# A four-layer graph network on one core: the scatters of the second edge sort dealt out over three stages, and the pair counting split differently between VectorE and ScalarE

## The chip, the cores and the metric

The kernel runs on one core of a Trainium2 chip. The metric is device time in microseconds (us), lower is better. Before the change three runs gave 10820.09, 10835.07 and 10841.47 us, median 10835.07 us.

The core has engines that run side by side and meet at semaphores: PE (TensorE, matrix products; its weight loads stand in a row of their own, PEld), DVE (VectorE), ACT (ScalarE), POOL (GpSimd) and SP (SyncE, which here only issues DMAs). POOL issues the indirect DMAs, in which a column of 128 indices in on-chip memory names the DRAM row of each of 128 elements. An indirect DMA that writes so is a scatter, one that reads so is a gather.

## The reference

The graph has 3125 nodes and 103,125 edges (50,000 random ones, their reverses, and a loop for each node). Four layers follow each other, each on relu(layer norm(x)), each added to x:

```python
edge_index = jnp.stack([src, dst])
x = x + L0(relu(layernorm(x)), ..., edge_index, edge_type_64)    # attention with a relation per edge, softmax over edges of one src
x = x + L1(relu(layernorm(x)), edge_index, ...)                  # 3 graph attention layers, softmax over edges of one dst
x = x + L2(relu(layernorm(x)), src, dst, ...)                    # 2 graph convolutions, then two small dense layers
x = x + L3(relu(layernorm(x)), ..., src, dst, edge_type_474)     # attention with a relation per edge, softmax over edges of one dst
```

In L1 each layer computes, for 4 heads,

```python
e = leaky_relu(alpha_s[src] + alpha_d[dst], 0.2)
alpha = softmax of e over the edges of one dst
out = segment_sum(xs[src] * alpha, dst) + b
```

and in L2 a convolution is `segment_sum(h[src], dst)`, with degrees as scales and a weight matrix. L1 and L2 need of the edges only how often each pair (node, node) occurs. L0 and L3 need the edges themselves, L0 sorted by src and L3 by dst.

## The kernel before, in words

Nodes are held as 25 blocks of 128 (`NB = 25`), edges as 816 tiles of 128 (`z.tiles = 816`). The program is a row of stages; between two stages all engines meet.

**Sorting (`group_edges`).** For each edge and for each of the two sorts q = 0 and 1 the place in a padded list of edges is worked out. For q = 0 POOL scatters the edges in the same stage (L244: 816 scatters of 128 elements of 8 bytes into `ells[0]`). For q = 1 the places only go to DRAM (`position_dram`), and `ells[1]` is filled later. `ells[1]` is first read in the last stage, L3.

**Counting (`count_pairs`).** It makes the 3200 x 3200 matrix of how often each pair of nodes has an edge, from `ells[0]`, and the logarithm of it, and writes both to DRAM (`counts`, `logs`). It goes over 13 pairs of node blocks (`PAIRS`), with buffer `p % 2` for pair p. For one pair and one group of 64 edge slots (in this run each pair has one group):

- DVE splits the ids into low and high parts (L1206 to L1215), PE transposes them, ACT copies them to `splitT` (L1131).
- DVE compares the high parts with 0..24 (`hi_hot`, L1220) and, for eight chunks of 16 rows, the low parts with 0..127 (`lo_hot`, L1224). In both the value from `splitT` is repeated along the innermost dimension.
- PE multiplies the one-hots of a chunk, 32 matmuls of 64 rows (L1107); DVE adds the product from PSUM to `counts[k]` (L1233), whose destination has a step of 256 elements innermost. POOL has cleared `counts[k]` before (L1075).
- PE then turns the counts of the pair in 50 transposes (L1088), ACT copies those out (L1138, 14 copies), sends them to DRAM (L1142), takes the logarithm (L1146) and, once DVE has clamped it (`tell`, L1243), sends `logs` (L1151).

The order is written out by hand. On ACT it is: `splitT` of pair p, copies and logarithm of pair p, `logs` of pair p - 1. On DVE: pair p + 1, then `tell(p)`. On PE: pair p, then turning pair p.

**L0.** It reads `ells[0]`; POOL gathers rows for it without pause. The change does not touch it.

**Attention layers (`graph_attention`, L1).** Three layers of 25 node blocks. POOL gathers the `logs` rows of a block (L1675, 1.6 MB into one of two buffers), which may start when DVE is through with the block two before. Then, for the first 68 of the 75 blocks, it issues 12 scatters of the second sort (L1682, `PART = 12`, 68 x 12 = 816); SP loads their indices and payload two parts ahead (L1660, L1661). DVE needs the `logs` of a block before it starts on it: for each of 4 heads one pass over 3200 elements that adds and takes the maximum (L1848) and one that adds the logs and finds the peak (L1852), which the trace names CUSTOM_DVE_ANT_0. ACT takes the exponentials (L1771) and copies what PE has transposed (L1779).

**Convolutions (`graph_convolution`, L2).** Twice PE multiplies the features by the count matrix (L2008), of which SP loads 25 blocks of 1.6 MB through a ring of four (L1983). POOL scatters x at the start (L704), waits until the first convolution has gone to DRAM (`second_out`), and gathers it in another order (L711).

## Time and profile before

The profiled execution took 10830.81 us, of which the span of the profile is 10829.0 us and 1.8 us lie around it. TensorE's mean granted clock is 0.77. Stages, from the same trace (busy us of each engine):

| stretch, us | stage | length | PE | DVE | ACT | POOL |
|---|---|---|---|---|---|---|
| 0 to 1493 | sorting | 1493 | 1076 | 1200 | 498 | 907 |
| 1493 to 2210 | counting | 717 | 182 | 570 | 164 | 76 |
| 2300 to 6020 | L0 | 3720 | 2330 | 2755 | 2291 | 2743 |
| 6150 to 8840 | attention layers, blocks | 2690 | 1876 | 2180 | 2056 | 2079 |
| 8895 to 9040 | first sum over the count matrix | 145 | 132 | 0 | 0 | 17 |
| 9115 to 9260 | second sum | 145 | 138 | 6 | 0 | 0 |
| 9330 to 10829 | L3 and output | 1499 | 906 | 1115 | 703 | 950 |

How to read it: a stage's busy engine is not by itself its bound. What ends the waits of that engine is asked of the waits and of the timeline. The page's own chain of waits names only the last hundredths of the span here, as all engines meet between stages.

### The profile page before, as it was taken

The numbers are of one execution on the slowest core, as the hardware profiler recorded it, in microseconds if no ns is written. First come the engines' busy times: TensorE is split into PE (matmuls) and PEld (weight loads), VectorE is DVE, ScalarE is ACT, GpSimd is POOL, SyncE is SP. The second block draws the span as 40 slices with busy tenths as digits, with TensorE's granted clock in tenths as the row PEclk, the third lists the DMA queues.
The fourth block names the chain that finished last, engine by engine and source line by source line (L and its number), as shares of the span: only waits on it lengthen the run. The fifth ranks groups of instructions, "written<-read, shape, count | busy, mean of one in ns | idle before, by whom it ended". The sixth has DMA issues, their size and how long they took to land. (4 is left out here: it accounts for less than half of the span.)

```text
span 10829.0 us, 223526 instructions
## 1 busy us (share of the span) xinstructions
PE 6746.9 (62%) x64938; PEld 5475.7 (51%) x64939; DVE 7986.2 (74%) x22059; ACT 5754.5 (53%) x12392; POOL 6921.5 (64%) x5770
## 2 busy tenths in 40 slices
PE   3984952236666566656666467676676668466665
PEld 2973952235554454545555355455554544366665
DVE  9779778847777677767777678778787870477776
ACT  4224222236666566646666477767777760155554
POOL 0777731057776777767777488868868710466665
PEclk8555555568887788778888798889898889777777
DMA  0111114322223223223222211111111126322222
GB/s 22 57 37 28 60 36 144 124 62 53 52 53 48 49 53 53 52 45 52 53 53 53 39 49 43 49 43 45 49 37 49 49 86 249 73 48 46 46 45 44
DMA packets 420007, 630.47 MB, mean 58 GB/s; under 512 B 273511, under 2 KB 330305, under 8 KB 396201
## 3 DMA queue, kind: packets, MB, share of 16 engines
q0 software_dynamic: 192432, 385.10, 17.0%
q1 hardware_dynamic: 160080, 158.87, 4.7%
q10 hardware_dynamic: 67401, 85.32, 2.2%
q8 instruction: 50, 0.82, 0.0%
q14 instruction: 44, 0.36, 0.0%
HBM read 527.43 MB, written 103.02 MB: 58 GB/s over the span
## 5 line engine op out<-in xcount | busy, mean ns | idle before, releaser
L895 POOL DMA_INDIRECT l_land<-table,l_words x3744 | 3596.3, 961 | 1342.5 <-issue 1158.6
L1682 POOL DMA_INDIRECT ell<-gat_stage_pay,gat_stage_at x816 | 1929.5, 2365 | 248.6 <-issue 248.6
L1365 PE MATMUL left_product_ps<-k_w,messageT 128*128 128x128 f32 x5616 | 1045.5, 343 | 530.2 <-ACT messageT L1400 530.2
L1365 PEld LDWEIGHTS left_product_ps<-k_w,messageT 128*128 128x128 f32 x5616 | 881.4, 239 | 736.6 <-ACT messageT L1400 736.6
L2231 PE MATMUL rel_ps<-relation_parts,hot 128*128 128x128 bf16 x11328 | 831.1, 248 | 414.8 <-DVE hot L2330 414.8
L1779 ACT COPY gat_probT<-gat_ps 128x512 f32<-128x512 f32 (+1 forms) x2100 | 1026.5, 550 | 112.8 <-PE gat_ps L1722 100.1
L2231 PEld LDWEIGHTS rel_ps<-relation_parts,hot 128*128 128x128 bf16 x11328 | 810.7, 114 | 436.2 <-DVE hot L2330 436.2
L244 POOL DMA_INDIRECT ell<-pay,position x816 | 842.4, 1032 | 289.3 <-issue 280.0
L1359 PE MATMUL left_turned_ps<-ident,message 128*128 128x128 f32 x2808 | 560.2, 334 | 725.4 <-DVE message L1491 725.4
L1722 PE MATMUL gat_ps<-ident,gat_logit 128*128 128x128 f32 x3750 | 629.7, 307 | 605.1 <-ACT gat_logit L1771 589.7
L1416 ACT ACTIVATE weighed<-kept,l_prob 128x128 f32 x2784 | 888.9, 391 | 59.1 <-ACT l_prob L961 59.0
L1722 PEld LDWEIGHTS gat_ps<-ident,gat_logit 128*128 128x128 f32 x3750 | 462.8, 155 | 765.1 <-ACT gat_logit L1771 618.3
L1359 PEld LDWEIGHTS left_turned_ps<-ident,message 128*128 128x128 f32 x2808 | 387.2, 173 | 826.7 <-DVE message L1491 823.7
L295 PE MATMUL looked_ps<-count,loT_wide 128*128 (+1 forms) x3264 | 755.6, 384 | 47.8 <-issue 44.8
L1351 PE MATMUL rel_ps<-relation_parts,hotT 128*128 128x256 bf16 x4248 | 777.3, 335 | 2.0 <-ACT hotT L1395 2.0
L295 PEld LDWEIGHTS looked_ps<-count,loT_wide 128*128 128x128 f32 x3264 | 744.7, 333 | 56.7 <-issue 54.2
L1412 ACT ACTIVATE right<-left_product_ps 128x512 f32<-128x512 f32 x702 | 418.1, 596 | 622.0 <-DVE l_score L1552 363.4
L1771 ACT ACTIVATE gat_logit<-gat_logit,gat_peak 128x1536 f32<-128x1536 f32 (+1 forms) x300 | 487.0, 1624 | 417.1 <-DVE gat_peak L1852 416.7
L1728 PE MATMUL gat_ps<-gat_probT,h 128*32 128x128 f32 x15000 | 706.4, 282 | 0.1
L981 DVE TENSOR_REDUCE part<-weighed 128x128 f32<-128x1024 f32 x348 | 667.2, 1917 | 27.1
L1722 PE MATMUL gat_ps<-ident,work 128*128 128x128 f32 x3750 | 574.9, 284 | 178.8 <-ACT work L1771 156.3
L1552 DVE CUSTOM_DVE_ANT_0 product<-right,left_now 128x128 f32<-128x128 f32 x2784 | 625.3, 288 | 8.6
(332 smaller groups left out, 15741.2 us busy)
## 6 DMA issues: line engine op xcount, KB each, us to landing
gcn_edges<-counts SPq DMA_DIRECT2D x50, 1600.0 KB, 8.1
l_land<-table,l_words POOLq DMA_INDIRECT x3744
rows<-low_dram SPq DMA_DIRECT2D x34, 1536.0 KB
counts<-pair_turned_sb ACTq DMA_DIRECT2D x12, 3200.0 KB, 9.4
logs<-pair_logs ACTq DMA_DIRECT2D x12, 3200.0 KB, 18.2
ell<-pay,position POOLq DMA_INDIRECT x816
ell<-gat_stage_pay,gat_stage_at POOLq DMA_INDIRECT x816
l_words<-ell SPq DMA_DIRECT2D x476, 8.0 KB
```

Source lines behind the costliest of these rows:

```text
L244: pool.indirect_dma_start(c.ells[0][:, :], bass.IndirectOffsetOnAxis(ap=position[:, 0, t:t + 1], axis=0), pay[:, t, :], None).then_inc(pla ...
L295: pe.matmul(looked_ps[r % HALVES][:, j, :], loT_wide[:, r % CAST, j, :], count[:, bass.ds(tile + j, 1), :].rearrange("p a n -> p (a n)"), ...
L895: pool.indirect_dma_start(self.land[:, p, s, :], None, table[:, :], bass.IndirectOffsetOnAxis(ap=self.words[:, p, s, 0:1], axis=0)).then_i ...
L1351: mm = pe.matmul(rel_ps[:, pair, :].rearrange("p s d -> p (s d)"), hotT[:, k * (H // 2) + j, :], parts[:, t, :, :].rearrange("p s d -> p ( ...
L1359: mm = pe.transpose(messageT_ps[:, k * H + j, :], message[:, k * H + j, :], c.ident[:, :])
L1365: mm = pe.matmul(right_ps[:, k * H + j, :], messageT[:, k, j, :], k_w[:, :], start=True, stop=True)
L1416: last = nc.scalar.activation(weighed[:, s, :], kept[:, bass.ds(n % 2, 1), s, :].rearrange("p a d -> p (a d)"), ACT.Copy, scale=soft.prob[ ...
L1682: pool.indirect_dma_start(c.ells[1][:, :], bass.IndirectOffsetOnAxis(ap=stage_at[n % 2][:, t:t + 1], axis=0), stage_pay[n % 2][:, t, :], N ...
L1722: mm = pe.transpose(ps[:, q % 4, r * P:(r + 1) * P], logit[t % 2][:, j * P:(j + 1) * P], c.ident[:, :])
L1728: mm = pe.matmul(ps[C * r:C * (r + 1), 4 + t % 2, 0:P], xs[:, 4 * q + r, t * C:(t + 1) * C], probT[:, q % 4 * 4 + r, :], start=(q == 0), s ...
L1779: nc.scalar.copy(probT[:, q % 4 * 4:q % 4 * 4 + rows_of(q), :].rearrange("p r d -> p (r d)"), ps[:, q % 4, 0:rows_of(q) * P]).then_inc(mov ...
L2231: mm = pe.matmul(rel_ps[:, k * H + s, :], hot[:, k, g, s, :], parts[:, g, t, :], start=(g == 0 and t == 0), stop=(g == PARTS - 1 and t == 2))
```

## The change

The 816 scatters of the second sort are dealt out over three stages: 144 in counting, 576 in the attention layers (8 behind each of 72 gathers, in place of 12 behind each of 68), and 96 in the convolutions, between the scatter of x and the wait for `second_out`. POOL's 13 clears of `counts` go.

In counting, the one-hots have the row innermost (`hi_hot` [25, 128], `lo_hot` [128, 16]), and are compared with two prepared patterns `hi_iota` and `lo_iota`, so that both inputs and the output of L1241 and L1245 run with step 1 in bf16. The matmuls now read their operands with a step (16 elements for `lo_hot`, 128 for `hi_hot`). For the first group of a pair ACT copies the product from PSUM into `counts` (L1145) and no addition is made; only further groups are added by DVE. Turning and finishing pair p come behind the counting of pair p + 1 on PE and ACT.

```diff
             @block.gpsimd
             def _(pool):
-                for p in range(PAIRS):
...
-                    nc.gpsimd.memset(counts[p % 2][:, :, :, :], 0.0).then_inc(cleared, 1)
+                pool.wait_ge(early_in, 32)
+                for t in range(EARLY_TILES):
+                    pool.indirect_dma_start(c.ells[1][:, :], bass.IndirectOffsetOnAxis(ap=early_at[:, t:t + 1], axis=0),
+                                            early_pay[:, t, :], None).then_inc(early_placed, 16)
+                pool.wait_ge(early_placed, 16 * EARLY_TILES)
...
-                                    mm = pe.matmul(chunk_ps[u % 2][:, b, j * NB:(j + 1) * NB], lo_hot[half, u % 2, j, :],
-                                                   hi_hot[half, u * CHUNK + j, :], start=True, stop=True)
+                                    mm = pe.matmul(chunk_ps[u % 2][:, b, j * NB:(j + 1) * NB], lo_hot[half, u % 2, :, j],
+                                                   hi_hot[half, :, u * CHUNK + j], start=True, stop=True)
...
+                        with act.If(g < 1):
+                            for u in range(CHUNKS_OF):
+                                act.wait_ge(counted, n * CHUNKS_OF + (u + 1))
+                                nc.scalar.copy(counts[k][:, :, :, u * CHUNK:(u + 1) * CHUNK].rearrange("p h b j -> p b j h"),
+                                               chunk_ps[u % 2][:, :, 0:CHUNK * NB]
+                                               .rearrange("p b (j h) -> p b j h", h=NB)).then_inc(kept, 1)
...
                 with act.Fori(0, PAIRS // 2 - 1) as two:
                     for k in range(2):
-                        pair(two * 2 + (k + 1), 1 - k, two + k)
+                        pair(two * 2 + (k + 2), k)
+                        finish(two * 2 + (k + 1), 1 - k, two + k)
                         tell(two * 2 + k, k)
...
-                for k in range(2):
-                    V.memset(logs[k][:, :, :, :], 0.0)
+                V.tensor_copy(hi_iota[:, :, :], spread(c.iota_rb[:, 0:NB], [P, NB, P], 2))
+                V.tensor_copy(lo_iota[:, :, :], spread(c.iota_rb[:, :], [P, P, CHUNK], 2))
...
-                        V.tensor_tensor(hi_hot[:, :, :], spread(c.iota_rb[:, 0:NB], [P, P, NB], 1),
-                                        spread(splitT[:, 1, :], [P, P, NB], 2), ALU.is_equal)
+                        V.tensor_tensor(hi_hot[:, :, :], hi_iota[:, :, :], spread(splitT[:, 1, :], [P, NB, P], 1),
+                                        ALU.is_equal)
...
-                            V.tensor_tensor(lo_hot[:, u % 2, :, :], spread(c.iota_rb[:, :], [P, CHUNK, P], 1),
-                                            spread(splitT[:, 0, u * CHUNK:(u + 1) * CHUNK], [P, CHUNK, P], 2),
+                            V.tensor_tensor(lo_hot[:, u % 2, :, :], lo_iota[:, :, :],
+                                            spread(splitT[:, 0, u * CHUNK:(u + 1) * CHUNK], [P, P, CHUNK], 1),
                                             ALU.is_equal).then_inc(hot_ready, 1)
...
-    PART = 12
-    PARTS = z.tiles // PART
+    PART = 8
+    PARTS = (z.tiles - EARLY_TILES - LATE_TILES) // PART
...
                 for n in range(2 * NB):
+                    if n == RING_OF:
+                        sp.dma_start(late_at[:, :], c.position_dram[:, late]).then_inc(late_in, 16)
+                        sp.dma_start(late_pay[:, :, :], a["payloads"][1][:, late, :]).then_inc(late_in, 16)
...
                 scatter_rows(pool, z, c.perms[0], c.table, x, x_out)
+                pool.wait_ge(late_in, 32)
+                for t in range(LATE_TILES):
+                    pool.indirect_dma_start(c.ells[1][:, :], bass.IndirectOffsetOnAxis(ap=late_at[:, t:t + 1], axis=0),
+                                            late_pay[:, t, :], None).then_inc(late_placed, 16)
                 pool.wait_ge(second_out, 16)
                 gather_rows(pool, z, c.perms[0], c.table_h, work, second_in)
+                pool.wait_ge(late_placed, 16 * LATE_TILES)
```

The order of instructions, at the three places that matter. First POOL, from the end of sorting to L0, and then at the start of the attention layers, before:

```order
L233 DMA perm_dram<-pairs,rank_i 3200x2 x25
...
L1075 MEMSET pair_counts 128x6400 x13
...
L711 DMA x<-in_x,perm 128x128 x25
...
L711 DMA gat_degree<-degree_dram,perm 128x1 x25
L1675 DMA gat_logs<-logs,perm 128x3200
L1682 DMA ell<-gat_stage_pay,gat_stage_at 13427712x2 x12
```

and now, with the place in the convolutions behind it:

```order
L233 DMA perm_dram<-pairs,rank_i 3200x2 x25
...
L1079 DMA ell<-early_pay,early_at 13427712x2 x144
...
L711 DMA x<-in_x,perm 128x128 x25
...
L711 DMA gat_degree<-degree_dram,perm 128x1 x25
L1702 DMA gat_logs<-logs,perm 128x3200
L1709 DMA ell<-gat_stage_pay,gat_stage_at 13427712x2 x8
...
L704 DMA table<-x,perm 3328x128 x25
L2033 DMA ell<-late_pay,late_at 13427712x2 x96
L711 DMA work<-table_h,perm 128x128 x25
```

POOL has 144 scatters where it had 13 clears, 8 behind a gather of logs where it had 12, and 96 more in the convolutions.

Next ACT in counting, one pair of the loop, before:

```order
L1131 CAST pair_splitT<-pair_split_ps 128x256
...
L1138 COPY pair_turned_sb<-pair_turned_ps 128x512 x6
L1138 COPY pair_turned_sb<-pair_turned_ps 128x128
...
L1142 DMA counts<-pair_turned_sb 128x2x3200
...
L1146 ACTIVATE pair_logs<-pair_counts,pair_few 128x6400
```

and now (the copy out of `pair_chunk_ps` stands eight times; the turned copies behind it are those of the pair before):

```order
L1141 CAST pair_splitT<-pair_split_ps 128x256
L1142 COMPARE_AND_BRANCH
L1144 ISA
L1145 COPY pair_counts<-pair_chunk_ps 128x2x16x25
...
L1156 COPY pair_turned_sb<-pair_turned_ps 128x512 x6
L1156 COPY pair_turned_sb<-pair_turned_ps 128x128
...
L1160 DMA counts<-pair_turned_sb 128x2x3200
...
L1164 ACTIVATE pair_logs<-pair_counts,pair_few 128x6400
```

Eight copies with a stepped destination have come onto ACT. They have left DVE, which had before:

```order
L1220 TENSOR_TENSOR pair_hi_hot<-iota_rb,pair_splitT 128x3200
L1224 TENSOR_TENSOR pair_lo_hot<-iota_rb,pair_splitT 128x2048 x2
L1231 ISA
L1233 TENSOR_TENSOR pair_counts<-pair_chunk_ps,pair_counts 128x2x16x25
L1224 TENSOR_TENSOR pair_lo_hot<-iota_rb,pair_splitT 128x2048
```

and has now, for the first group of a pair:

```order
L1241 TENSOR_TENSOR pair_hi_hot<-pair_hi_iota,pair_splitT 128x3200
L1245 TENSOR_TENSOR pair_lo_hot<-pair_lo_iota,pair_splitT 128x2048 x2
L1251 COMPARE_AND_BRANCH
L1253 ISA
L1245 TENSOR_TENSOR pair_lo_hot<-pair_lo_iota,pair_splitT 128x2048
```

Between two comparisons DVE has only a wait left.

## Rows read from the trace of the kernel before

**Rows 1.** Busy time by stretch: us, busy (instructions) by engine, clock, DMA share, GB/s.

```profile
1493.00:2210.00 717.00, 181.69 (x3979) 139.75 (x3979) 570.23 (x352) 164.22 (x202) 76.30 (x19) 0.59 0.34 117
6150.00:8840.00 2690.00, 1875.55 (x23337) 1380.22 (x23338) 2179.90 (x1069) 2055.57 (x3621) 2079.26 (x865) 0.90 0.17 46
```

**Rows 2.** Waits in the attention stage: us in total, times, longest.

```profile
DVE gat_logit L1848 <- DMA gat_logs<-logs,perm: 351.7, 36, 17.0
DVE gat_logit L1848 <- PE gat_ps L1722: 46.5, 37, 2.3
```

**Rows 3.** Timeline of POOL there: start, us, engine, line, operation, [idle before <- releaser].

```profile
7556.70 3.30 POOL L1682 DMA_INDIRECT ell<-gat_stage_pay,gat_stage_at  x1 [0.30 <-issue]
7560.31 3.17 POOL L1682 DMA_INDIRECT ell<-gat_stage_pay,gat_stage_at  x1 [0.31 <-issue]
...
7597.19 0.96 POOL L1682 DMA_INDIRECT ell<-gat_stage_pay,gat_stage_at  x1 [0.30 <-issue]
```

**Rows 4.** Timeline of DVE there; a block starts at L1848 gat_logit<-...,x.

```profile
7559.10 3.55 DVE L1848 SCALAR_TENSOR_TENSOR work<-gat_source_row,gat_own,gat_low_row 128x3200 f32<-128x3200 f32 x1
...
7602.49 3.55 DVE L1848 SCALAR_TENSOR_TENSOR gat_logit<-gat_source_row,gat_own,x 128x3200 f32<-128x3200 f32 x1 [7.73 <-DMA gat_logs<-logs,perm]
...
8145.62 3.55 DVE L1848 SCALAR_TENSOR_TENSOR gat_logit<-gat_source_row,gat_own,x 128x3200 f32<-128x3200 f32 x1 [14.62 <-DMA gat_logs<-logs,perm]
...
8601.03 3.55 DVE L1848 SCALAR_TENSOR_TENSOR gat_logit<-gat_source_row,gat_own,x 128x3200 f32<-128x3200 f32 x1
...
8808.93 3.55 DVE L1848 SCALAR_TENSOR_TENSOR gat_logit<-gat_source_row,gat_own,x 128x3200 f32<-128x3200 f32 x1
...
8837.45 0.08 DVE L1852 DVE_READ_ACCUMULATOR2_ANT gat_peak<- 128x1 f32 x1
```

**Rows 5.** DVE's L1220 in counting: duration min/median/max, first and last start.

```profile
L1220 DVE TENSOR_TENSOR pair_hi_hot<-iota_rb,pair_splitT x13: 3491/3492/3493, 1523.7 to 2139.5; 128x3200 bf16<-128x3200 bf16 x13
```

**Rows 6.** Timeline of one pair in counting, and the next stage's first gather.

```profile
1576.43 3.49 DVE L1220 TENSOR_TENSOR pair_hi_hot<-iota_rb,pair_splitT 128x3200 bf16<-128x3200 bf16 x1 [14.76 <-ACT pair_splitT L1131]
1579.84 4.49 DVE L1224 TENSOR_TENSOR pair_lo_hot<-iota_rb,pair_splitT 128x2048 bf16<-128x2048 bf16 x2
1582.18 0.61 PE L1107 MATMUL pair_chunk_ps<-pair_hi_hot,pair_lo_hot 64*128 64x25 bf16 x32 [11.61 <-DVE pair_lo_hot L1224]
...
1610.79 6.83 DVE L1243 SCALAR_TENSOR_TENSOR pair_logs<-pair_logs 128x6400 f32<-128x6400 f32 x1 [0.37 <-issue]
...
1611.98 0.59 ACT L1138 COPY pair_turned_sb<-pair_turned_ps 128x512 f32<-128x512 f32 x1 [35.59 <-PE pair_turned_ps L1088]
...
1621.73 5.63 ACT L1146 ACTIVATE pair_logs<-pair_counts,pair_few 128x6400 f32<-128x6400 f32 x1 [0.63 <-ACT pair_turned_sb L1138]
...
2202.49 0.98 POOL L711 DMA_INDIRECT x<-in_x,perm  x1 [108.86 <-PEq L2419]
```

**Rows 7.** Groups of instructions in counting: busy us, mean ns, idle before.

```profile
L1224 DVE TENSOR_TENSOR pair_lo_hot<-iota_rb,pair_splitT 128x2048 bf16<-128x2048 bf16 x104 | 237.7, 2296 | 0.0
L1233 DVE TENSOR_TENSOR pair_counts<-pair_chunk_ps,pair_counts 128x800 f32<-128x800 f32 x104 | 177.7, 1723 | 0.0
...
L1107 PEld LDWEIGHTS pair_chunk_ps<-pair_hi_hot,pair_lo_hot 64*128 64x128 bf16 x3328 | 52.5, 102 | 418.0 <-DVE pair_lo_hot L1224 418.0
...
L1196 DVE MEMSET pair_logs<- 128x6400 f32 x2 | 10.8, 5392 | 3.0 <-issue 3.0
```

**Rows 8.** Two groups elsewhere: ACT with a stepped operand, DVE at two elements a cycle.

```profile
L344 ACT ACTIVATE count<-count,first_slot 128x816 f32<-128x816 f32 x12 | 21.6, 1949 | 31.8 <-DVEq L493 31.8
...
L1890 DVE TENSOR_SCALAR x<-gat_source_row 128x3200 f32<-128x3200 f32 x3 | 5.5, 1827 | 0.3
```

**Rows 9.** The largest DMAs that ACT issues: count, size, us to landing.

```profile
logs<-pair_logs ACTq DMA_DIRECT2D x12, 3200.0 KB, 18.2
```

**Rows 10.** Timeline of POOL in the first convolution.

```profile
8916.06 0.96 POOL L704 DMA_INDIRECT table<-x,perm  x1 [0.30 <-issue]
...
9083.35 0.98 POOL L711 DMA_INDIRECT work<-table_h,perm  x1 [166.33 <-DMA table_h<-res]
```

More of the change, by code:

```diff
@@ L989, with count_pairs @@
 FEW = 2.0 ** -60
[L992 removed]
+EARLY_TILES, LATE_TILES = 144, 96
+def count_pairs(nc, top, z, c, a):
     NB = z.blocks
@@ L997, in count_pairs @@
     CHUNKS_OF = P // CHUNK
+    assert PAIRS % 2 and PAIRS > 4 and NB % 2
     with ExitStack() as ctx:
@@ L1081, in turn_counts @@
                 def turn_counts(p, k, parts):
-                    pe.wait_ge(summed, p + 1)
+                    many, first = steps(pe, p)
+                    pe.wait_ge(kept, (first + many) * CHUNKS_OF + 2)
                     for b in range(parts):
@@ L1124, in _, with pair @@
                     act.sem_inc(done, 16)
-                def pair(p, k, earlier, parts=2):
+                def pair(p, k):
                     many, first = steps(act, p)
@@ L1246, in _ @@
                 pair(0, 0)
-                with v.Fori(0, PAIRS // 2) as two:
+                pair(1, 1)
+                with v.Fori(0, PAIRS // 2 - 1) as two:
                     for k in range(2):
-                        pair(two * 2 + (k + 1), 1 - k)
+                        pair(two * 2 + (k + 2), k)
                         tell(two * 2 + k, k)
-                tell(PAIRS - 1, 0)
+                pair(PAIRS - 1, 0)
+                for p in range(PAIRS - 3, PAIRS):
+                    tell(p, p % 2)
 def attention_over_relations(nc, top, z, c, a, x, h, res, work):
```

70 lines of the change are left out of this document (41 added, 29 removed).

## The prediction, made before the changed kernel was run

> **What bounds the kernel now.** I read the profile in this order: busy time by stage, then the waits inside the stages that the change touches, then the timelines that show how these waits come about. All engines meet between stages, so a stage's length is its own matter and the changes add up. Two stages carry the change: counting (717 us, DVE busy 570) and the attention layers (2690 us, DVE busy 2180) [rows 1].
>
> In the attention stage DVE waits 351.7 us for the `logs` of its block, in 36 waits, and 46.5 us more for PE [rows 2]. The logs are late because POOL, which issues their gather behind 12 scatters, is full. The timelines show how. A scatter that POOL starts while DVE is in a long pass takes 3.30 us: started at 7556.70, it ends at 7560.00, 0.9 us after DVE went from one pass to the next at 7559.10. The next takes 3.17 us. While DVE stands still one takes 0.96 us [rows 3, 4]; with the 0.30 us between two, 1.27. So one POOL DMA goes through per DVE pass. A block has 8 long passes. The last block, with no scatter beside it, runs from 8808.93 to 8837.53, 28.6 us; I use 28.5, 3.56 per pass. Thirteen blocks with scatters, 8145.62 to 8601.03, take 35.0 us each [rows 4].
>
> This closes numerically: two blocks need 2 x 13 = 26 POOL DMAs. Sixteen go in the 57.0 us of the passes, ten while DVE stands, 10 x 1.27 = 12.7, together 69.7 us against 70.0 measured.
>
> In counting the pairs follow each other by (2139.5 - 1523.7) / 12 = 51.3 us [rows 5]. The path alternates. DVE makes the one-hots and adds (1576.43 to about 1610.8); then PE and ACT turn the counts and ACT takes the logarithm, from 1611.98 to 1621.73 + 5.63 = 1627.36, while DVE only clamps the logs before (6.83 us) and splits the next ids, and then waits for `splitT`, which stands behind the logarithm on ACT [rows 6].
>
> **The change part by part.**
>
> *Attention layers.* Two blocks now need 18 POOL DMAs: 16 in the passes, two while DVE stands, 2.5 us, so 59.5 us per two blocks, 1.25 us of wait per block in place of 6.5. The 398 us of rows 2 are 61 blocks at 6.5, so some blocks (those behind each projection, where POOL gets ahead) don't wait today. With 72 blocks to scatter in, 61/68 of them is 65 blocks, and 65 x 1.25 = 81 us at most. POOL gains on DVE wherever DVE does something short, and now needs little, so I take 65 us. Gain 398 - 65 = 333 us; bounds 300 (wait of 1.5 per block in all) and 398 (none left).
>
> *Counting, DVE.* Per chunk DVE has a comparison (2296 ns) and an addition (1723 ns) [rows 7]; the addition goes. The comparison keeps its 2048 elements, but nothing is repeated innermost any more. No row shows a two-input bf16 comparison in this form. It lies between 2.20 us from start to start as now (rows 6: 4.49 for two) and the rate of two elements a cycle that DVE reaches in L1890, 3200 in 1827 ns [rows 8], that is 1.17 us for 2048 and 1.83 for `hi_hot` in place of 3.49. I take the lower, since the repeated operand is what differs from L1890's plain rows. If it stays, the price is under the rivals.
>
> Rows 7 show 2296 ns for the comparison with a repeated innermost operand. The Trainium skill ("VectorE: DVE Perf Modes", "The perf-mode tier table (the rule you actually need)") has `tensor_tensor` in bf16 from SBUF at two elements a cycle, 1224 ns at 2048; by it the comparison is worth what I take, by the row of today nothing. The trace has no instruction of that form.
>
> *Counting, ACT.* It gets eight copies of 800 elements from PSUM with a destination step of 256 elements. Below lies the plain rate: 512 elements in 0.59 us [rows 6], some 0.86 for 800. Above lies L344, 816 elements in 1949 ns with steps on both sides [rows 8]. The nearest row is DVE's own addition with this very source and destination, 1.72 us [rows 7], and I take that, 1.82 with the wait at its start.
>
> *Counting, PE.* 32 matmuls take 0.61 us [rows 6], and a weight load of 128 columns 52.5 / 3328 = 15.8 ns of engine time [rows 7]. Now both operands are read with a step. The steps of rows 7 and 8 cost the other engines about a factor of two (1723 ns for 800 elements against 2296 for 2048), so I take 1.2 us per chunk. That is under ACT's 1.82 and shows only in the first chunk of a pair.
>
> Rows 7 show 15.8 ns for 128 columns, several columns a cycle. The Trainium skill has two rules that differ here. "TensorE: Matmul & The Clock Gate" ("Weight-path perf modes — Fast Weight Load (FWL) and DoubleRow") has the fast load work on packed and stepped columns alike, by which the chunk stays at 0.61. "SBUF — State Buffer" ("Door 1: The DMA port swizzle (why `[64,N]` ≈ `[32,N]`)") has each access that leaves a 16-byte line pay, free steps ending at 8 bf16, and here the steps are 16 and 128; it gives no size for PE. It is the reason behind the first and the last rival; this trace has no stepped PE operand.
>
> *Counting, the new path.* ACT is now the chain. Per pair: `splitT` and its handover 0.8; then it waits for `hi_hot` 1.8, the first `lo_hot` 1.2, the first chunk 1.2 and handovers 0.2, together 4.4; eight copies at 1.82, 14.5; branches 0.5: 20.2. Finishing a pair: 1.5 until PE has turned the first rows, then 1611.98 to 1627.36, 15.4: 16.9. Thirteen pairs 263, twelve finishes 203, the last half pair 8, the first ids 4, at the end the clamp 6.8 and the last logs DMA, 12: 497 us. DVE's part of a pair (3 us of splitting, 1.8 + 8 x 1.2 of comparing, 6.8 of clamping, 21) fits beside it. The start: two clears of `logs` (10.8 [rows 7]) become two copies of about 4, so counting begins at 1514 instead of 1520.7. It ends at 2011 against the 2202.5 at which the next stage's first gather starts [rows 6]: gain 190. Bounds: 100 (ACT 1.95 and PE 2.1) and 265 (ACT 0.86, PE 0.61).
>
> *What is hidden there.* The 144 scatters are under 144 x 1.5 = 216 us in a stage of 500, with short DVE instructions between which they pass. The logs DMA takes 18.2 us [rows 9] against 37 per pair. POOL's clears were beside DVE's work and give nothing.
>
> *Convolutions.* POOL is through with x at 8916.06 + 0.96 and then waits until 9083.35 [rows 10]. 96 scatters at 1.27, 122 us, end at 9039, 44 us before. If that cover went (scatters of 1.8 us), the second sum would start later. The two loads of indices go ahead of the fifth block of counts: 3 us lost.
>
> **The sum.** 10830.8 (the profiled execution; the median of the runs is 4 us above) - 333 - 190 + 3 = 10311; predicted median about 10,310 with that spread.
>
> **The rivals.**
> - *PE's stepped operands set the pace of counting.* For: both steps are new. At 2.1 us per chunk a pair is longer by 8 x 0.43 + 0.9 = 4.3, in all 56: 10,365. At 3.4, 16 x 13 = 208: 10,520. Against: today's chunk leaves room for a factor of three.
> - *The comparisons stay at one element a cycle.* Then DVE paces at 2.20: 8 x 0.38 + 1.7 + 1.0 = 5.8 per pair, 75 in all: 10,385.
> - *POOL loses a whole pass.* If the ninth DMA costs 3.56 instead of 1.27, a block takes 32.0, 65 x 3.5 = 230 of the 398 stay: 10,475. Against: between blocks DVE has a short copy and waits, and the count for 26 DMAs closed.
> - *Slower than before: PE's weights come in column by column at the stepped rate.* L344 has (1949 - 280) / 816 = 2.05 ns per element [rows 8]; 128 columns are 262 ns, a chunk 8.4 us, a pair 8 x 6.7 + 7.2 = 61 longer, 793 in all: 11,100. It decides from about 6.3 us per chunk, ten times today's.
> - *The change doesn't do what it says*: a first group that isn't the only one would bring DVE's additions back. The 13 `hi_hot` of 13 pairs [rows 5] exclude it; the place in the attention stage is sure.
>
> **How the numbers follow.** Forecast (10,195 to 10,370 from the bounds above: ACT at 0.86 gives 54 less, no wait left 65 less; ACT at 1.95 and a gain of 300 give 57 more) 0.68. Stepped PE operands 0.14, comparisons unchanged 0.05, a whole pass lost 0.10, column by column 0.03. The range 10,200 to 10,460 leaves out the slow half of the first rival, most of the third and the last, and a little below. A run can tell 0.2%, 22 us. Only the last case is slower; about no change needs a chunk near 6.3 us, 0.01. Faster 0.96, same 0.01, slower 0.03.
>
> **What would show it.** In the profile of the changed kernel: the waits of L1848's successor for the logs at 40 to 80 us, blocks near 29.5 us; starts of `hi_hot` some 37 us apart; `lo_hot` at 1.2 us; L1145 at 1.7 us; 32 matmuls in 1.2 us; POOL waiting for `second_out` for about 40 us. The forecast is wrong if PE's weight loads of `lo_hot` last longer than ACT's copies, if DVE still waits over 150 us for logs, or if counting is longer than 560 us.

## The result and the profile after

The changed kernel takes 10463.44 us (median of 4 runs, 10451.36 to 10470.67) against 10835.15 us before (4 runs); the ratio is 0.9656, 95% interval 0.9644 to 0.9667. It is faster, as forecast, but by 372 us where 525 were forecast, and it lies 3 us above the range.

Two groups of chips appear in what follows. On the "quick" chips the kernel before takes 10,823 to 10,835 us, on the "slow" chips 13,588 to 13,724. On a slow chip sorting ends near 2,470 us in place of 1,513, L0 takes some 1,200 us more, the attention stage 40 to 80 more, and L3 2,035 us in place of 1,573. What makes these chips slow is open. Without scatters beside them, the loops of counting and both sums over the count matrix take the same time on either. So lengths of those stretches can be compared across chips, and whole times only as ratios to the kernel before on the same chip.

Two words of the profile come up often. "issue" is idle time for which the profile shows nothing that the engine waited for; "remote" is a wait whose end it can put down to no instruction.

The stretches after, in the columns of [rows 1]: counting, the attention blocks, first sum over the count matrix, second sum.

```profile
1493.00:2030.00 537.00, 257.63 (x3979) 215.37 (x3979) 255.88 (x248) 323.85 (x306) 175.73 (x144) 0.59 0.71 150
5998.00:8368.00 2370.00, 1843.13 (x23338) 1346.37 (x23339) 2175.38 (x1068) 2050.11 (x3621) 1879.67 (x633) 0.96 0.17 52
8421.00:8681.00 260.00, 152.60 (x350) 69.51 (x350) 0.81 (x2) 0.00 (x0) 109.83 (x115) 0.78 1.02 188
8751.00:8888.00 137.00, 136.68 (x350) 63.46 (x350) 0.26 (x1) 0.00 (x0) 0.00 (x0) 0.98 0.69 252
```

The first sum stands out: 260 us for the same 350 matmuls that took some 150 before, at 188 GB/s, with the DMA engines busy throughout.

**Attention.** The waits that answer to [rows 2], and DVE's first and last block start:

```profile
DVE gat_logit L1875 <- PE gat_ps L1749: 48.2, 24, 7.1
DVE gat_logit L1875 <- DMA gat_logs<-logs,perm: 37.9, 15, 5.9
...
L1875 DVE SCALAR_TENSOR_TENSOR gat_logit<-gat_source_row,gat_own,x x75: 3543/3548/3621, 6000.2 to 8336.8; 128x3200 f32<-128x3200 f32 x75
```

86 us of waits are left of 398. From the first block to the end of the last (8336.8 + 28.5) it is 2365 us, against 2684 (6153.8 to 8837.5) before: 319 us gained. A block takes 29.7 us on average where it took 34.2; in both figures the two steps from one layer to the next, 96 to 99 us each, are left out.

**Counting.** What answers to [rows 5, 7], and the waits of ACT:

```profile
L1241 DVE TENSOR_TENSOR pair_hi_hot<-pair_hi_iota,pair_splitT x13: 1824/1826/1826, 1512.3 to 1977.4; 128x3200 bf16<-128x3200 bf16 x13
...
L1145 ACT COPY pair_counts<-pair_chunk_ps 128x800 f32<-128x800 f32 x104 | 160.1, 1660 | 82.1 <-PE pair_chunk_ps L1114 56.7 <-remote 25.4
...
L1245 DVE TENSOR_TENSOR pair_lo_hot<-pair_lo_iota,pair_splitT 128x2048 bf16<-128x2048 bf16 x104 | 124.7, 1223 | 34.1 <-PE pair_chunk_ps L1114 21.8 <-remote 12.3
...
ACT pair_logs L1164 <- DMA logs<-pair_logs: 60.4, 4, 29.3
...
logs<-pair_logs ACTq DMA_DIRECT2D x1, 3200.0 KB, 69.7
```

`lo_hot` takes 1.22 us, ACT's copy 1.66. The starts of the 13 `hi_hot` are 19.0, 35.8, 39.3, 69.9, 40.0, 62.4, 32.7, 33.4, 32.5, 33.0, 33.2 and 33.9 us apart. POOL's 144 scatters run from 1498.2 to 1747. So an undisturbed pair needs 33 us, and while the scatters run some need 60 to 70. The last line is the DMA of `logs` at 1600.64: it lands after 69.7 us, in [rows 9] after 18.2, and ACT waits for it with the next logarithm. The next stage's first gather starts at 2043.9, 158.6 us earlier than before; L0 takes 5 us of that back, and the attention layers' first block starts 153.6 us earlier.

**First sum.** PE in the middle of it, before and after (start, us, engine, line, operation, [idle before <- releaser]):

```profile
8939.56 20.80 PE L2008 MATMUL gcn_ps<-gcn_edges,work 128*128 128x512 f32 x54
```

```profile
8482.63 7.11 PE L2046 MATMUL gcn_ps<-gcn_edges,work 128*128 128x512 f32 x14 [32.90 <-DMA gcn_edges<-counts]
8497.92 7.99 PE L2046 MATMUL gcn_ps<-gcn_edges,work 128*128 128x512 f32 x14 [8.18 <-DMA gcn_edges<-counts]
```

Before, the matrix is there when PE wants it; after, PE waits for one block after the other. The waits of PE from 8421 to 8680; in the same stretch before (8893 to 9045) the first line stood at 59.6 us:

```profile
PE gcn_ps L2046 <- DMA gcn_edges<-counts: 153.5, 10, 47.1
```

One wait of 47 us, near the start of the sum, stands in every version. GB/s in 40 slices of the first sum, before and then after:

```profile
GB/s 414 443 402 413 34 48 34 54 205 348 424 438 421 421 299 332 421 434 424 399 392 353 290 329 350 247 307 360 240 297 388 219 297 360 272 282 385 282 269 367
```

```profile
GB/s 423 416 283 35 35 59 110 190 142 176 91 134 176 83 145 59 49 52 71 29 71 120 118 190 75 223 235 81 225 160 335 394 376 335 301 276 294 343 329 272
...
ell<-late_pay,late_at POOLq DMA_INDIRECT x96, 40.4
```

POOL's late scatters go from 8444.7 to 8565.6, and the last take up to 65 us to land. From 8440 to 8616 the rate is 29 to 235 GB/s. A packet of 12,800 bytes of the count matrix takes 1.48 us on average between 8446 and 8616, the longest 13; before it took 0.54. PE goes from 8421.1 to 8679.8, 258.7 us, where before it went from 8892.9 to 9044.8, 151.8.

### The profile page after: what moved, and what is told of

It is laid out like the page before. It is cut to its first block and busy times, and to the rows that moved or that the text cites. A ratio compares the mean times of both kernels' runs of the same rounds, so it can differ in the third digit from the quotient of the medians.

```text
span 10460.8 us, 223670 instructions
## 1 busy us (share of the span) xinstructions
PE 6797.4 (65%) x64938; PEld 5515.9 (53%) x64939; DVE 7667.5 (73%) x21955; ACT 5908.6 (56%) x12496; POOL 6911.8 (66%) x5757
## 5 line engine op out<-in xcount | busy, mean ns | idle before, releaser
L1709 POOL DMA_INDIRECT ell<-gat_stage_pay,gat_stage_at x576 | 1665.0, 2891 | 175.5 <-issue 175.5
L1749 PE MATMUL gat_ps<-ident,gat_logit 128*128 128x128 f32 x3750 | 602.9, 296 | 317.5 <-ACT gat_logit L1798 299.4
L1749 PEld LDWEIGHTS gat_ps<-ident,gat_logit 128*128 128x128 f32 x3750 | 433.8, 148 | 480.7 <-ACT gat_logit L1798 334.9
L353 ACT CAST loT_wide<-loT 128x512 f32<-128x512 bf16 x408 | 252.1, 618 | 700.8 <-PE looked_ps L299 672.0
## 6 DMA issues: line engine op xcount, KB each, us to landing
logs<-pair_logs ACTq DMA_DIRECT2D x12, 3200.0 KB, 18.2
```

Of the source, the lines that this page charges most:

```text
L1709: pool.indirect_dma_start(c.ells[1][:, :], bass.IndirectOffsetOnAxis(ap=stage_at[n % 2][:, t:t + 1], axis=0), stage_pay[n % 2][:, t, :], N ...
L1749: mm = pe.transpose(ps[:, q % 4, r * P:(r + 1) * P], logit[t % 2][:, j * P:(j + 1) * P], c.ident[:, :])
```

## The experiments

Lengths in this table are from the traces: counting from the first to the last start of `hi_hot`, the sums from PE's first to its last start in them. The kernels late_row, late_wide, reads2 and plain2 have two runs each, the other changed ones four.

| kernel | chip | us | ratio to before | counting | 1st sum | 2nd sum |
|---|---|---|---|---|---|---|
| before | quick | 10835 | 1 | 615.8 | 151.8 | 136.4 |
| changed | quick | 10463 | 0.9656 | 465.1 | 258.7 | 136.4 |
| again | slow | 13224 | 0.9738 (0.9720 to 0.9756) | 560.3 | 244.2 | 136.1 |
| no_late | slow | 13281 | 0.9674 (0.9658 to 0.9691) | 558.3 | 151.8 | 137.2 |
| no_early | slow | 13181 | 0.9605 (0.9589 to 0.9621) | 381.0 | 248.8 | 137.4 |
| no_both | slow | 12954 | 0.9532 (0.9509 to 0.9554) | 381.3 | 150.5 | 136.0 |
| bare | slow | 12954 | 0.9517 (0.9501 to 0.9533) | 381.5 | 153.3 | 137.3 |
| count_alone | slow | 13454 | 0.9797 (0.9780 to 0.9814) | 382.5 | 150.3 | 136.3 |
| late_reads | slow | 13384 | 0.9753 (0.9737 to 0.9770) | 557.3 | 247.2 | 136.2 |
| reads2 | slow | 13230 | 0.9718 (0.9699 to 0.9737) | 562.2 | 246.5 | 136.2 |
| late_row | slow | 13252 | 0.9746 (0.9727 to 0.9766) | 559.1 | 248.1 | 136.0 |
| late_wide | slow | 13228 | 0.9729 (0.9710 to 0.9748) | 556.3 | 246.5 | 136.2 |
| late_plain | slow | 13138 | 0.9666 (0.9648 to 0.9684) | 558.0 | 154.1 | 137.2 |
| plain2 | slow | 13143 | 0.9654 (0.9635 to 0.9673) | 558.0 | 153.6 | 136.4 |
| gaps | slow | 13241 | 0.9745 (0.9727 to 0.9764) | 559.9 | 151.5 | 137.4 |
| deal7 | slow | 13249 | 0.9734 (0.9718 to 0.9750) | 755.9 | 151.7 | 137.2 |
| deal9 | slow | 13236 | 0.9733 (0.9717 to 0.9749) | 556.9 | 151.6 | 137.4 |
| deal10 | slow | 13239 | 0.9750 (0.9726 to 0.9773) | 451.7 | 151.1 | 135.9 |
| paced | quick | 10453 | 0.9652 (0.9636 to 0.9668) | 452.6 | 210.8 | 178.5 |
| deal8 | quick | 10379 | 0.9587 (0.9571 to 0.9603) | 490.6 | 151.3 | 135.8 |

### Which scatters cost: no_late, no_early, no_both, bare, count_alone, again

```diff
-                for t in range(LATE_TILES):          # no_late, no_both, bare
-                    pool.indirect_dma_start(c.ells[1][:, :], ..., late_pay[:, t, :], None).then_inc(late_placed, 16)
-                for t in range(EARLY_TILES):         # no_early, no_both, bare
-                    pool.indirect_dma_start(c.ells[1][:, :], ..., early_pay[:, t, :], None).then_inc(early_placed, 16)
-EARLY_TILES, LATE_TILES = 144, 96                    # count_alone: all 816 in the attention layers
+EARLY_TILES, LATE_TILES = 0, 0
-    PART = 8
+    PART = 12
```

no_late: 

> The changed kernel without the 96 scatters of the convolutions (these 96 tiles never reach the second sorted list; their indices and payload are still loaded). Theory T (the many small writes of the scatters slow every other transfer that runs beside them, here the 1.6 MB blocks of the count matrix, far beyond the time that their own packets show): the stretch from the last attention block to the end falls back from 2094.8 us to the 1991.5 us of before, so about 10,360 us, packets of 12800 B near 0.5 us from the first one on. Rival R1 (the slow stretch comes from something else that the change brought in there: the loads of indices and payload in front of the fifth block, the order on SP's queue): 10,450 to 10,465 us. Rival R2 (POOL's place in the order is what costs, the gather behind second_out starts late): the gather starts when second_out is written in both, so no more than 10 us would come back.

no_early: 

> The changed kernel without the 144 scatters in counting (these tiles never reach the second sorted list; indices and payload are still loaded). Theory T: the pairs that took 62 to 70 us and the 36 to 40 us ones come down to the 33 us of the undisturbed ones: last hi_hot at 1513 + 12 x 33.3 = 1913 in place of 1978, about 65 us saved, 10,398 us, and the logs of a pair land in 18 us throughout. Rival R3 (the slow pairs come from the new order on ACT, where the logarithm of a pair waits for the logs of the pair two before, whatever else runs): the slow pairs stay, 10,455 to 10,465 us. The stages behind it stay as they are in both.

count_alone: 

> The counting edit alone: one-hots with the row innermost, ACT's copies, pairs one ahead, and all 816 scatters of the second sort in the attention layers as before (12 behind each of 68 gathers). Theory T: counting runs undisturbed, pair period 33 us, last hi_hot near 1913, 2202.5 - 1950 = about 250 us saved there and nothing elsewhere: 10,585 us. Rival R3 (slow pairs by ACT's order): about 190 us, 10,645 us. Both have attention blocks of 35 us as before.

again: 

> The changed kernel itself, unchanged, as the base for the three kernels beside it and for the four runs before, which were taken on a chip on which the kernel before took 13,724 us in place of 10,835. If this is the quick chip: 0.966 of before, first sum over the count matrix 250 to 260 us long. If it is the slow one: no_early took 13,181 us there with the late scatters and no_late 13,281 us with the early ones, so with both about 13,385 us; first sum 249 us as in no_early, first pair of counting 193 us as in no_late. If it comes out at 13,281 us or less on the slow one, the late scatters cost nothing at the end and the stretched first sum is made good somewhere behind it.

no_both: 

> Neither the 96 scatters of the convolutions nor the 144 of counting (these tiles never reach the second sorted list). If the two costs lie in different stages and add up (theory T): first sum 152 us, counting 360 to 385 us from the first hi_hot to the last; on the quick chip 10,463 - 107 - 84 = 10,272 us, on the slow one about 100 us under no_early, 13,080 us. If they overlap in a common cause (R4: the loads of the indices, which are still made), less than 120 us in all.

bare: 

> The kernel of no_both once more (no scatters in counting and none in the convolutions; these tiles never reach the list), for the quick chip, where the forecast was made. Theory T (the two losses read from the trace add up): 10,463 - 107 - 84 = 10,272 us, ratio 0.948; first sum 152 us, counting 380 us between the first and the last hi_hot, all pairs near 33 us. If the slow pairs come from ACT's order: counting 440 us or more.

Without the late scatters the first sum is back at 151.8 us, though the loads of their indices and payload stayed: theory T holds in place and size, and R1 and R2 fall. On the quick chip deal8, which has no late scatters either, shows the same: 151.3. GB/s of no_late's first sum:

```profile
GB/s 424 423 419 425 194 30 43 63 193 371 415 428 432 392 290 405 428 428 425 402 261 308 352 271 274 341 355 251 305 375 261 268 341 325 262 308 351 274 281 325
```

Without the early ones every pair behind the first takes 32 to 34 us, on the three slow chips on which this was run. So ACT's new order costs nothing (R3 falls). Since undisturbed pairs take 33 us on the quick chip too, 381.5 serves as base there, and the changed kernel lost 465.1 - 381.5 = 84 us of counting to 144 scatters; paced, with the same 144 and on a quick chip too, lost 71 (452.6). In no_late and again the first pair alone takes 193 to 197 us in place of 17, and the same 144 cost 177 to 179 us; these waits of again between 2460 and 3040 (in bare the first line stands at 24.1 us) show that PE stands idle for "issue" before one after another of the 32 matmuls of a chunk, and DVE and ACT behind it:

```profile
PEld pair_chunk_ps L1114 <- issue: 196.2, 147, 4.1
DVE pair_lo_hot L1245 <- remote: 180.8, 5, 88.4
ACT pair_counts L1145 <- remote: 179.2, 5, 88.1
```

The two losses add up: again less no_both is 269 us, their parts 179 + 94 = 273. The totals named for the quick chip can't be held against these runs, all of them taken on slow chips. The two named for a slow chip missed by 161 us (again: 13,385) and 126 us (no_both: 13,080), but the kernel before is itself 135 us faster on the chip on which both ran than on the one that they were worked out from. As ratios they hold: 0.9753 forecast for again against 0.9738, 0.953 for no_both against 0.9532.

### What in a late scatter costs: late_reads, late_plain, late_row, late_wide, reads2, plain2

```diff
-                    pool.indirect_dma_start(c.ells[1][:, :], bass.IndirectOffsetOnAxis(ap=late_at[:, t:t + 1], axis=0),
-                                            late_pay[:, t, :], None)
+                    pool.indirect_dma_start(late_pay[:, t, :], None, c.ells[1][:, :],        # late_reads, reads2, late_row
+                                            bass.IndirectOffsetOnAxis(ap=late_at[:, t:t + 1], axis=0))
+                    pool.dma_start(late_pay[:, t, :], c.ells[1][t * P:(t + 1) * P, :])       # late_plain, plain2
+                nc.gpsimd.tensor_scalar(late_at[:, :], late_at[:, :], 1.0 / 32, None, ALU.mult)   # late_wide, before the loop
+                    pool.indirect_dma_start(late_wide[:, t, :], None, late_rows, ...)        # late_wide, 64 words each
+                nc.gpsimd.iota(late_at[:, :], pattern=[[P, LATE_TILES]], base=0, channel_multiplier=1)   # late_row
```

late_reads: 

> The changed kernel with the 96 scatters of the convolutions turned round: with the same indices, in the same place and as often, POOL gathers 8 bytes per index from the second sorted list (these tiles never get into it). Theory T1 (writes of 8 bytes to DRAM are what slows the others): close to the kernel without them, 10,360 to 10,385 us, 12800 B packets near 0.5 us. Theory T2 (the number of descriptors is what slows the others, reading or writing): as the changed kernel, 10,450 to 10,465 us.

late_plain: 

> The changed kernel with each of the 96 late scatters turned into a plain DMA on POOL's queue, which reads 128 elements of 8 bytes that lie in a row in the second sorted list into the 128 partitions (these tiles never get into the list). late_reads, with indices, stretched the first sum to 247 us (152 without). Theory T3 (the count of small elements on the DMA engines is what slows the others): the first sum stays at 230 to 260 us. Theory T4 (what slows the others comes with indices: POOL making the descriptors of an indirect DMA): first sum 152 to 165 us, and the kernel about 100 us under the changed one.

late_row: 

> The changed kernel with the 96 late scatters turned into gathers of 8 bytes by index, as in late_reads, but the indices are consecutive rows (96 tiles x 128 rows in a row, made by an iota), so that the same bytes are fetched as by the plain DMAs of late_plain, which left the first sum at 154 us. These tiles never get into the list. Theory T6 (an indexed DMA of 8-byte elements slows the others whatever its addresses): first sum 235 to 260 us. Theory T5 (it is the random addresses in DRAM): first sum 150 to 170 us.

late_wide: 

> The changed kernel with the 96 late scatters turned into gathers by index (the random positions divided by 32) of 256-byte elements: as many indices and elements, 32 times the bytes (3.1 MB, at the 320 GB/s of the undisturbed first sum 10 us). These tiles never get into the list. Theory T6a (each indexed DMA slows the others, whatever the size of its elements): first sum 240 to 270 us. Theory T7 (only small elements do: beside the indexed writes of x, with 512 bytes, the count matrix kept on coming at 414 to 443 GB/s): first sum 155 to 180 us.

reads2: 

> The kernel of late_reads once more (the 96 late scatters as indexed gathers of 8 bytes), for the quick chip. On the slow chip the first sum was 247 us, with the 12800-byte packets at 0.5 to 0.6 us and PE starting one matmul per 2.8 us; with writes the packets took 1.2 to 3.2 us. Theory P1 (each indexed DMA takes its microsecond): first sum 235 to 260 us here too. Theory W (on the quick chip, where PE's issue was not slowed, only writes cost, by the packets they slow): 150 to 170 us.

plain2: 

> The kernel of late_plain once more (the 96 late scatters as plain DMAs of 128 elements of 8 bytes in a row), for the quick chip: 150 to 160 us for the first sum as on the slow one (154 us), if what costs comes with indices; 235 us or more if on the quick chip it is the small elements.

All six ran on slow chips. There, reading instead of writing, consecutive rows instead of random ones, 256 bytes instead of 8: the first sum stays at 246 to 248 us. With plain DMAs of as many 8-byte elements on the same queue it is 154. T1, T3, T5 and T7 fall for the slow chips: what costs there is a run of DMAs with indices. PE and GB/s in late_reads' first sum:

```profile
10922.36 1.01 PE L2046 MATMUL gcn_ps<-gcn_edges,work 128*128 128x512 f32 x1 [1.79 <-issue]
10925.16 1.01 PE L2046 MATMUL gcn_ps<-gcn_edges,work 128*128 128x512 f32 x1 [1.79 <-issue]
...
10927.96 1.01 PE L2046 MATMUL gcn_ps<-gcn_edges,work 128*128 128x512 f32 x1 [1.79 <-issue]
...
GB/s 424 423 349 23 49 218 362 222 149 117 1 1 1 1 52 309 171 1 1 1 1 265 1 0 0 0 372 429 432 383 351 318 310 295 306 289 306 332 314 318
```

One matmul starts per 2.8 us, idle for "issue", while the DMA engines move 1 GB/s: the data are there and PE does not get its instructions. Writes by index do the same on a slow chip; PE's waits in the first sum of again (10729 to 10974):

```profile
PE gcn_ps L2046 <- issue: 85.3, 31, 30.3
PE gcn_ps L2046 <- DMA gcn_edges<-counts: 46.5, 1, 46.5
```

In the changed kernel on the quick chip PE has no such idle time. It waits for data, because packets are slow. The packets part the runs in another way than the chips do. Beside late writes a 12,800-byte packet takes 1.5 us on average on either kind of chip (changed 1.48, again 1.45, no_early 1.67). Beside late reads (late_reads 0.56, late_row 0.54, late_wide 0.54) and plain reads (late_plain 0.54) it takes what it takes without any. So there are two effects: PE's issue held up, seen on slow chips with any DMAs by index, and slow packets, seen with writes alone. With one of them or both, 96 late DMAs by index cost 93 to 107 us. Which property of the writes slows the packets was not tested, and on a quick chip neither reads by index nor plain DMAs were run: there it is shown that the 96 scatters cost, and not that the cost comes with their indices.

The Trainium skill ("DMA: Bandwidth & Descriptors", "Specifications") puts the smallest transfer at line rate at 512 bytes and has the DMA engines read, modify and write below it. As the cause of PE's held issue it does not fit: reads by index cost as much as the writes, and so do 256-byte ones, and plain 8-byte reads cost nothing. For the slow packets it stands as an untested rival. Plain 8-byte writes were not run, but every version has plain 4-byte writes, and the trace of the kernel before speaks for it. There 25 indexed writes of x, of 512 bytes an element, go from 8882.5 to 8917.0. Their 4,096-byte packets take 0.16 us each until near 8909 the plain DMA of `order_dram` starts, over 3,000 writes of 4 bytes. Then the same packets of x take 0.8 us on average, and 1.3 in the 8 us behind it. (The rate of 34 to 54 GB/s at that time says little, since SP issues no block of the matrix until the writes have landed.)

### Where the scatters could stand: gaps, paced, deal7 to deal10

```diff
+                pool.wait_ge(gap_in, 32)                       # gaps: in L0, 72 in place of the late ones
+                fill(range(FIRST_GAP))                         # 32 before its first scatter of rows
...
+                fill(range(FIRST_GAP, LATE_TILES))             # 40 behind its last gather
-                for t in range(LATE_TILES):                    # paced: for part 0 and 1, around the gather
+                    for j in range(LATE_TILES // 4):
+                        pool.wait_ge(edges_used, part * NB + j + 1)
...
-EARLY_TILES, LATE_TILES = 144, 96                              # PART = 8
+EARLY_TILES, LATE_TILES = 216, 0                               # deal8, PART = 8, 75 parts
+EARLY_TILES, LATE_TILES = 291, 0                               # deal7, PART = 7
+EARLY_TILES, LATE_TILES = 141, 0                               # deal9, PART = 9
+EARLY_TILES, LATE_TILES = 66, 0                                # deal10, PART = 10
```

gaps: 

> A whole version: nothing is scattered in the convolutions. 144 tiles in counting and 8 behind each gather of the attention layers as now, but for all 75 (600 tiles), and the last 72 in two places in which POOL and the DMA engines idle: 32 before the first layer's scatter of its rows (36 us idle there) and 40 behind its last gather (60 us idle). Theory T (scatters cost where other DMAs or a streaming PE run beside them, and nothing elsewhere): first sum 152 us, up to 15 us lost in the first gap (32 x 1.26 = 40 us against 36, and their landing), nothing in the second, three more attention blocks with scatters at 3 us each: 10,463 - 107 + 25 = about 10,380 us on the quick chip, 80 us or more under the changed kernel on either. Rival R5 (a scatter costs its microsecond wherever it stands): 72 + 24 in place of 96 scatters, so the time stays within 20 us of the changed kernel.

deal9: 

> A whole version with another deal: 141 tiles in counting, 9 behind each of the 75 gathers of the attention layers (675), none in the convolutions. From the blocks of before and after (12 scatters 35.0 us, 8 scatters 31.5 us, none 28.5 us) a ninth costs 0.9 us in each of 72 blocks, and the three last blocks get 4 us each: +77 us in the attention layers, -94 to -107 us in the first sum. Theory T (the prices add up): 15 to 30 us under the changed kernel, ratio to before 0.971 to 0.973 where the changed kernel had 0.9738. If the ninth one is covered as the eighth: 0.966.

deal10: 

> A whole version: 66 tiles in counting, 10 behind each of the 75 gathers (750), none in the convolutions. Against the changed kernel: +144 us in the attention layers for the ninth and tenth at 0.9 us each and 15 us for the last three blocks, -94 us in the first sum, and counting gives back its price per scatter: 78 x 1.24 = 97 us where counting lost 179 us to 144 scatters, 45 us where it lost 84. Theory T: about 30 us under the changed kernel on a chip like the last two, ratio 0.971; rival: more scatters in front of the logs of the next block bring back DVE's wait for them, blocks over 33.3 us, ratio 0.976 and above.

paced: 

> A whole version: the 96 late scatters stay in the convolutions, but POOL waits for PE's next block of the count matrix before each two of them: 48 in the first sum (24 blocks), 48 in the second. Theory P1 (each indexed DMA takes about its own microsecond from what runs beside it, however they are spaced): the two sums together stay about 95 us longer than without scatters (152 + 137), some 50 us each, and the time within 15 us of the changed kernel, 0.974 of before. Theory P2 (a long run of indexed DMAs back to back is what shuts the others out, and single ones pass): each sum within 10 us of 152 and 137 us, and the kernel 75 to 95 us under the changed one, 0.967.

deal8: 

> A whole version: 216 tiles in counting, 8 behind each of the 75 gathers, none in the convolutions. If the price in counting stays at 1.24 to 1.39 us per scatter (179 us for 144, 109 us for 78 on the slow chips): +95 us in counting, +20 us in the attention layers for the last three blocks, -94 us in the first sum: 20 us over the changed kernel, 0.975. If further scatters in counting fall beside loops that no longer notice them (the pairs behind the first one kept their 33 us): 0.967 to 0.969.

deal7: 

> A whole version one step on from deal8: 291 tiles in counting, 7 behind each of the 75 gathers (525), none in the convolutions. On the quick chip 72 more scatters in counting (216 in place of 144) cost 25.5 us, 0.35 us each; 8 scatters make an attention block 3.0 us longer than none (31.5 against 28.5). If the eighth is worth the mean of the eight (0.37 us): -28 us there, +26 us in counting, no gain over deal8 (10,379 us, 0.9587). If it is worth what the ninth to twelfth are (0.9 us): -66 + 26 = -40 us, 0.955. If counting runs out of room (291 x 1.22 = 355 us of POOL against 490 us): 0.960 and above. On a slow chip: as deal8 or worse, 0.98.

*paced* gives each sum 48 scatters, two per block: 210.8 and 178.5 us, 59 and 42 longer than before. Spread or in a row, 96 cost 101 to 107 us (P1). The scatters land in 11.9 us here (40.4 in the changed kernel), and still the blocks take 25.1 (8.6 without), a 12,800-byte packet 0.96 on average:

```profile
gcn_edges<-counts SPq DMA_DIRECT2D x25, 1600.0 KB, 25.1
...
ell<-late_pay,late_at POOLq DMA_INDIRECT x48, 11.9
```

*gaps* won the first sum back (151.5 us) and lost it in L0: from counting to the first `logs` gather it took 5267 us, in again 5173. I had misread both gaps. They lie between two stages, where all engines have met; the scatters stood inside the stage. The first 32 take 39 us and POOL comes to its own first scatter 34 us later than in again; the last 40 take 50 us, behind its last gather, and hold up the meeting at the end. So R5's number came true, not T's: 17 us over again, forecast within 20.

*deal9 and deal10* on slow chips are the changed kernel's equals; deal9 comes out as T has it. Beside again, 99 more scatters in the attention stage cost 110 us, 174 cost 214, and 78 fewer in counting gave back 109: 1.1 to 1.4 us each. *deal7*: 51 fewer in attention give 90 us, 1.8 each, 147 more in counting cost 196, 1.3 each. These are differences between chips: the attention stage with one and the same deal took 2522 to 2543 us on the chips of again, no_early, no_late and bare and up to 2552 on that of deal9, so the prices there are good to 0.1 to 0.4 us. In deal10 DVE waits 174.6 us for `logs`, in again 47.5: its rival came nearer than T.

*deal8* on the quick chip is faster than both kernels: 10378.64 us (4 runs), and its interval of the ratio lies clear of the changed kernel's. Both forecasts for it missed, having priced counting from slow chips. 72 more scatters in counting cost 25.5 us against the changed kernel and 38 against paced on the same chip, 0.35 to 0.53 each. Three more attention blocks with scatters show no cost (2470 us from the first gather to the first sum, 2471 in the changed kernel, 2481 in paced), and the first sum has its rate back:

```profile
8442.00:8595.00 153.00, 140.56 (x350) 64.91 (x350) 0.55 (x1) 0.00 (x0) 18.18 (x19) 0.93 0.93 318
```

On a slow chip it was not run. By deal7's price there, 1.3 us, 72 more in counting would cost an estimated 96 us, as much as the first sum gives back. Whether deal7 gains on a quick one is open; on the slow chip it came out at 0.9734 where its text says 0.98.

The forecasts for deal7, deal9 and deal10 go by blocks of 35.0, 31.5 and 28.5 us. The 31.5 has the steps between layers in it. Without them eight scatters make a block 1.2 us longer, not 3.0: 0.16 us each.

## Why the prediction was wrong, step by step

- **Convolutions: the step that failed.** I wrote "96 scatters at 1.27, 122 us, end at 9039, 44 us before ... 3 us lost". POOL's side was right: the scatters take 121 us and end at 8565.6, and POOL still waits for `second_out`, 152.8 us, of which the longer sum made 107. But I asked only whether POOL has the time, not who else lives on what it uses. The sum beside it is fed at 317 GB/s by DMAs, and with the 96 scatters it took 107 us more, where the prediction has 3. No rival of mine had it. no_late gives it back on a slow chip and deal8 on a quick one. That it comes with the indices is shown for slow chips alone (late_plain); on the quick chip, for which the forecast was made, the packets are slow and their cause stays open.
- **Counting: mis-sized twice.** Gain 158.6 us up to the next stage's first gather and 153.6 up to the attention layers, forecast 190. The pair without scatters takes 33 us, not 37: ACT's eight copies start 1.54 us apart, not 1.82, which is 2.2 of the 4 us. That alone would have made the gain some 237. "The 144 scatters are under 216 us in a stage of 500" had the same fault as above, a price of nothing because POOL has the time: they cost 84 us. `logs` lands after up to 69.7 us in place of 18.2 (60.4 us of waits of ACT), and PE's matmuls are idle for "issue" for 13.4 us, 1.4 in no_early.
- **The comparisons and PE's steps: right.** `lo_hot` 1223 ns (forecast 1.17 to 1.2), `hi_hot` 1826. The Trainium skill's 1224 ns for this form ("VectorE: DVE Perf Modes", "The perf-mode tier table (the rule you actually need)") agrees. 32 matmuls take 1.20 to 1.24 us (forecast 1.2), a weight load 121.4 / 3328 = 36.5 ns where it was 15.8, at the same mean granted clock of the stage, 0.59. So stepped operands do cost PE, a factor of 2.3 in the loads and 2 in the chunk, and stay under ACT's pace; the first, second and last rival fall. Of the two rules that the prediction cites, the run goes with the one by which stepped accesses pay. A chunk at 0.61 did not come.
- **Attention: right.** 86 us of waits left (forecast 65), a block 29.7 us (forecast near 29.5), 319 us gained (forecast 333); no whole pass is lost.
- The sum: 10,311 + 104 (convolutions) + 36 (counting) + 14 (attention) - 3 (L3, 1573 in place of 1577) = 10,462 against 10,462.6 of the profiled execution.

## What to carry to other kernels

An instruction that fits into an engine's idle time is not free by that: ask also what its transfers take from the stage around it, and above all from a stage whose engine is fed by large DMAs without slack. Here an indexed DMA of 128 elements cost 0.35 to 1.8 us nearly wherever it was put. The cheapest places were in loops with slack: the first eight per attention block (29.7 us against 28.5, 0.16 each) and counting on the quick chip. A gap in front of a stage is no room for work that is placed inside it. And a test that takes the cost away on one chip need not name its cause on another: look whether the waits beside it are the same ones.

## What was not expected of the hardware

- Writes by index on POOL's queue slow others far beyond what their own packets show: the scatters' packets of 64 bytes are recorded at 0.015 us each, while the 12,800-byte packets beside them go from 0.54 to 1.5 us on average. Reads by index leave them at 0.54 to 0.56. Why is open. The 25 indexed writes of x, of 512 bytes an element, do no harm: beside them the rate is 402 to 443 GB/s (first four slices before). The 4-byte writes of `order_dram`, a plain DMA, do: beside and behind them a packet of x takes 0.8 to 1.3 us in place of 0.16.
- On the slow chips DMAs by index hold up PE's issue, to one matmul in 2.8 us, in late_reads with the DMA engines all but idle. Whether reads by index would cost as much on a quick chip is open: reads2 was meant for one and ran on a slow one.
- The price in counting depends on the chip: 0.35 to 0.58 us per scatter on quick chips (deal8, the changed kernel), 1.24 to 1.39 on slow chips (again, deal10).
